# Routed tokens sent to their experts' regions while the gates run, in place of gathers during the routed blocks

## What is computed

```python
t = layernorm(h).reshape(-1, 128)                     # 3136 tokens of 128 numbers
hs = gelu(einsum('td,nfd->ntf', t, sw1) + sb1)        # 2 shared experts, 512 hidden units, every token
shared = einsum('ntf,ndf->td', hs, sw2) + sb2.sum(0)
probs = softmax(t @ gate_w.T + gate_b)                # 8 routed experts
top_v, top_i = top_k(probs, 2)                        # each token goes to 2 of them
hr = gelu(einsum('td,efd->etf', t, rw1) + rb1)
oe = einsum('etf,edf->etd', hr, rw2) + rb2
out = h + shared + einsum('etd,te->td', oe, cw)       # cw: top_v at top_i, else 0
```

## Time and profile before

| | |
|---|---|
| median of the runs | 507.42 us |
| profiled execution | 508.58 us |
| its span (first to last instruction) | 506.8 us |
| PE busy | 386.9 us (76%) |
| DVE busy | 183.7 us (36%) |
| ACT busy | 208.2 us (41%) |
| POOL busy | 193.4 us (38%) |
| mean granted clock of TensorE | 0.891 of full |

### The profile page before, as it was taken

How to read it: one execution, slowest core, us unless ns; L and a number is a source line. 1 busy time by engine, 2 the same in 40 slices (tenths; PEclk the granted TensorE clock), 3 DMA queues, 4 the chain that set the end, 5 groups by cost and what they waited for, 6 DMA issues and landing times.

```text
span 506.8 us, 7360 instructions
## 1 busy us (share of the span) xinstructions
PE 386.9 (76%) x2561; PEld 313.5 (62%) x2561; DVE 183.7 (36%) x564; ACT 208.2 (41%) x423; POOL 193.4 (38%) x254
## 2 busy tenths in 40 slices
PE   0869998999589754999699978888596797696600
PEld 0648666666367643877589677777396496496600
DVE  0661858486930354435861111111021111121146
ACT  2641758463352143766333322424232342342243
POOL 6050262624110025400003466676546666556600
PEclk9995999999779795999988997999798998998955
DMA  9950349300225102110201234344334343444176
GB/s 222 262 160 2 97 120 321 118 1 10 87 77 167 45 1 65 32 34 1 104 38 18 55 130 141 136 141 176 90 119 140 125 147 135 134 130 136 70 210 176
DMA packets 35240, 55.43 MB, mean 109 GB/s; under 512 B 5431, under 2 KB 20397, under 8 KB 35209
## 3 DMA queue, kind: packets, MB, share of 16 engines
q1 hardware_dynamic: 30185, 46.25, 28.7%
q0 software_dynamic: 4480, 8.46, 6.6%
q10 hardware_dynamic: 544, 0.33, 0.3%
HBM read 28.63 MB, written 7.46 MB: 71 GB/s over the span
## 4 chain that ended last, share of the span: by engine, by line
PE 34%; issue 30%; DVE 10%; POOL 6%; POOLq 6%; DMA 5%; another core or an unknown queue 4%; ACT 3%; SPq 1%; DVEq 1%; ACTq 0%
PE bank L1459 12%; PE bank L1481 11%; PE bank L1469 4%; DVE dT L822 3%; DMA out<-osb 2%; DMA gbb<-in_L_ffn_gate_b 2%; ACT gf L765 2%; PE bank L1504 2%; POOLq L598 1%; POOL QT L566 1%; PE bank L1515 1%; POOLq L548 1%; POOL rstd L544 1%; DVE xtok L871 1%
## 5 line engine op out<-in xcount | busy, mean ns | idle before, releaser
L765 ACT ACTIVATE gf<-bank,wba 128x256 f32<-128x256 f32 x128 | 55.2, 474 | 99.0 <-remote 45.5
L610 POOL DMA_INDIRECT xg<-yd,take x64 | 62.5, 977 | 76.9 <-DVE give L1143 57.7
L617 POOL DMA_INDIRECT rd<-og,give x64 | 63.4, 990 | 63.3 <-DVE og L1155 47.1
L1481 PE MATMUL bank<-wbb,gf 128*128 128x128 f32 x512 | 69.1, 293 | 23.2 <-issue 23.1
L1481 PEld LDWEIGHTS bank<-wbb,gf 128*128 128x128 f32 x512 | 65.4, 206 | 25.5 <-issue 25.5
L1459 PE MATMUL bank<-x,wba 128*128 128x256 f32 x256 | 67.5, 406 | 14.0 <-issue 12.5
L1459 PEld LDWEIGHTS bank<-x,wba 128*128 128x128 f32 x256 | 49.4, 205 | 25.2 <-issue 17.0
L765 ACT ACTIVATE gf<-bank,vcol 128x392 f32<-128x392 f32 x64 | 34.7, 589 | 52.2 <-PE bank L1441 33.7
L1155 DVE TENSOR_TENSOR og<-bank,wbb 128x256 f32<-128x256 f32 x32 | 13.6, 424 | 101.8 <-remote 67.1
L1469 PE MATMUL bank<-gf,ws 128*128 128x392 f32 x128 | 45.1, 495 | 0.0
L1254 PE MATMUL bank<-patchT,Wp 128*128 128x392 f32 x96 | 37.4, 515 | 0.0
(11 more groups left out here) (242 smaller groups left out, 617.0 us busy)
## 6 DMA issues: line engine op xcount, KB each, us to landing
wbb<-stb SPq DMA_DIRECT2D x32, 320.0 KB
Xc<-in_x SPq DMA_DIRECT2D x12, 784.0 KB, 6.6
wba<-sta SPq DMA_DIRECT2D x32, 258.0 KB
rk<-rd SPq DMA_DIRECT2D x16, 196.0 KB
Tt<-kpad SPq DMA_DIRECT2D x8, 300.1 KB
raw<-in_L_ffn_rw SPq DMA_DIRECT2D x1, 2048.0 KB, 10.6
yd<-ym SPq DMA_DIRECT2D x8, 196.0 KB
out<-osb SPq DMA_DIRECT2D x8, 196.0 KB
```

Of the source, the lines that this page charges most:

```text
L610: G.indirect_dma_start(out=xg[i % AHEAD][:, t, :], out_offset=None, in_=yd[:, :], in_offset=bass.IndirectOffsetOnAxis(ap=take[:, at:at + 1 ...
L617: G.indirect_dma_start(out=rd[:, :], out_offset=bass.IndirectOffsetOnAxis(ap=give[:, at:at + 1], axis=0), in_=og[i % 2][:, t, :], in_offse ...
L765: nc.scalar.activation(gf[q % 2][:, o, 0:width(q)], bank[o][:, 0:width(q)], ACT.Gelu, bias=bias1(n, o)).then_inc(act_done, 1)
L1481: last = MM(bank[7][:, D * t:D * (t + 1)], gf[q % 2][:, o, 128 * t:128 * (t + 1)], wbb[i % WB][:, o * D:(o + 1) * D], start=o == 0, stop=o ...
```

## The change

The order of units is now all 16 shared units, then the 32 blocks. The sorting is done in four rounds of 8 pairs (`GPP`), in iterations 0 to 3, each as soon as its two groups' gates are through: `choose(g)` finds the two experts of each token from the logits alone, PE's `count(g)` numbers them, and `send(g)`, one iteration later, writes row numbers `xrow`. POOL's `dispatch(g)` then sends the rows of `ym` (now 8 buffers, one per group) to regions of `xd` in DRAM, one region of 3392 rows per expert: 16 indirect DMAs of 98 rows in each round, 64 in all. `number_slots` in iteration 5 finds each block's expert and its first row (`rowint`), and from there on `one_hots`, `invert` and `slot_tokens` work as before for `give` alone, one iteration later than before. SP clears 256 rows behind each region's end (`pad_rows`) and loads each block's 256 consecutive rows with one plain DMA (`load_tokens`). The gathers, the table `take` and the stores to `yd` are gone. The exponential of the gates is moved to iteration 6 and the routed weights to iteration 10 (`shares`).

The diff, cut to its core:

```diff
-LEAD = 12
-EVERY = 6
-ORDER = list(range(LEAD))
-for _i in range(NB):
-    ORDER.append(NSH + _i)
-    if _i % EVERY == EVERY - 1 and LEAD + _i // EVERY < NSH:
-        ORDER.append(LEAD + _i // EVERY)
+ORDER = list(range(NSH + NB))
...
-S_EXP = 4
-S_COUNT = 6
-S_HOT = 5
-S_TURN = 8
+S_NUMBER = 5
+S_HOT = 6
+S_TURN = 9
...
@@ SP
-            for c in range(NG):
-                store_y(c)
+            def load_tokens(i):
+                at = sp_.value_load(rowint[0:1, i:i + 1], min_val=0, max_val=E * TT - BLK)
+                if i == 0:
+                    sp_.wait_ge(st_pad, 16 * E)
+                    for g in range(NGR):
+                        sp_.wait_ge(dispatched[g], 16 * 2 * GPP)
+                if i >= AHEAD:
+                    sp_.wait_ge(tin_done, i - AHEAD + 1)
+                sp_.dma_start(xg[i % AHEAD][:, :, :], xd[bass.ds(at, BLK), :].rearrange("(t p) d -> p t d", t=TILES_OF)).then_inc(ld_xg[i % AHEAD], 16)
...
+            for e in range(E):
+                pad_rows(e)
...
+            for i in range(WB):
+                load_weights(i)
+            for i in range(WB - 1):
+                load_tokens(i)
             for i in range(NB):
-                load_weights(i)
+                if i + WB - 1 < NB:
+                    load_tokens(i + WB - 1)
+                if i + WB < NB:
+                    load_weights(i + WB)
...
@@ POOL, sort_constants
                 G.memset(nothing[:, :], 0.0)
+                G.memset(zrows[:, :, :], 0.0)
+                G.memset(keep[:, :, 1:GPP + 1], 1.0)
+                for i in range(2):
+                    G.memset(run[i][:, :, 0:1], 0.0)
+                for e in range(E):
+                    G.memset(base_of[:, e:e + 1], float(e * TT))
+                G.memset(keep[:, :, 0:1], 0.0)
                 G.memset(allone[:, :], 1.0).then_inc(sort_const, 1)
...
-            def gather(i):
+            def dispatch(g):
+                pool.wait_ge(row_ready, g + 1)
+                for c in range(GC * g, GC * (g + 1)):
+                    for p in range(GP):
+                        for k in range(2):
+                            at = GP * c + p
+                            G.indirect_dma_start(out=xd[:, :], out_offset=bass.IndirectOffsetOnAxis(ap=xrow[:, k, at:at + 1], axis=0),
+                                                 in_=ym[c][:, p, :], in_offset=None).then_inc(dispatched[g], 16)
...
@@ ACT
-                if c >= 4:
-                    act.wait_ge(y_T, c - 3)
-                    act.wait_ge(st_y[c % 4], 16 * (c // 4))
...
-                if q == S_EXP:
+                if q == S_NUMBER + 1:
                     act.wait_ge(lg_ready, 1)
-                    nc.scalar.activation(pr[:, :, :], lg[:, :, :], ACT.Exp).then_inc(exp_ready, 1)
+                    nc.scalar.activation(pr[:, :, :], lg[:, :, :], ACT.Exp)
+                    nc.scalar.activation(cwk[:, :, :], tops[:, :, :], ACT.Exp).then_inc(exp_ready, 1)
...
@@ DVE
-                if q == NG // 2 - 1:
-                    gate_logits()
-                    gate_probs()
-                    gate_second()
-                    sort_places()
+                if 1 <= q <= NGR:
+                    send(q - 1)
+                if q < NGR:
+                    choose(q)
+                if q == S_NUMBER:
+                    number_slots()
...
@@ PE
             def gate(c):
                 pe.wait_ge(yh_ready, c + 1)
+                if c % GC == 0 and c >= GC:
+                    pe.wait_ge(lg_read, c // GC)
+                if c >= 2 * GC and c % GC == 0:
+                    pe.wait_ge(row_ready, c // GC - 1)
...
+                if 1 <= q <= NGR:
+                    count(q - 1)
+                if q == NGR + 1:
+                    count_all()
```

More of the change, by code:

```diff
@@ L169, in tower @@
         rbb = place("rbb", [128, E, D], "w")
+        zrows = place("zrows", [128, TILES_OF, D], "w")
+        ymw = [place(f"ymw{i}", [PAIR, GP, D], "w") for i in range(4)]
         assert end["w"] <= base + SA, (end["w"] - base, SA)
@@ L200, in tower @@
         step256 = place("step256", [PAIR, NCNT], "y")
-        nothing = place("nothing", [PAIR, E * NPAIR], "y")
+        nothing = place("nothing", [PAIR, E], "y")
         idf = place("idf", [PAIR, NPAIR], "y")
@@ L245, in tower @@
         Av = [place(f"Av{i}", [PAIR, NQ, JG], "g", F16) for i in range(2)]
-        ym = [place(f"ym{i}", [PAIR, GP, D], "g") for i in range(4)]
-        first = place("first", [PAIR, E, NPAIR], "g")
+        ym = [place(f"ymg{i}", [PAIR, GP, D], "g") for i in range(4)] + ymw
         more = place("more", [PAIR, E, NCNT], "g")
         owner = place("owner", [1, NB, E], "g")
+        offs = place("offs", [1, NB, E], "g")
+        mine = place("mine", [1, E], "g")
         assert end["g"] <= base_h, (end["g"], base_h)
@@ L302, in tower @@
         ld_wb = [sem(f"ld_wb{i}") for i in range(WB)]
-        gathered = [sem(f"gathered{i}") for i in range(AHEAD)]
+        ld_xg = [sem(f"ld_xg{i}") for i in range(AHEAD)]
         scattered = [sem(f"scattered{i}") for i in range(2)]
@@ L307, in tower @@
         st_zero, st_k, st_out = sem("st_zero"), sem("st_k"), [sem(f"st_out{i}") for i in range(2)]
-        st_y = [sem(f"st_y{i}") for i in range(4)]
+        dispatched = [sem(f"dispatched{i}") for i in range(NGR)]
+        st_pad = sem("st_pad")
         lsrep_ready, par_T, ls_T, vec_T = sem("lsrep_ready"), sem("par_T"), sem("ls_T"), sem("vec_T")
@@ L1094, in sort_places @@
+                V.tensor_tensor(offs[:, :, :], colc[0:1, :].unsqueeze(2).broadcast_to([1, NB, E]),
+                                blocks[0:1, :].unsqueeze(1).broadcast_to([1, NB, E]), ALU.is_ge)
+                dve.drain()
                 V.tensor_reduce(ownsum[:, :], owner[:, :, :], AX.X, ALU.add)
-                V.scalar_tensor_tensor(shiftby[:, :], blocks[:, :], float(BLK), start, ALU.mult, ALU.subtract)
+                V.tensor_tensor(offs[:, :, :], offs[:, :, :], owner[:, :, :], ALU.subtract)
@@ L1106, in sort_places @@
+                dve.drain()
+                for k, of_ in enumerate((eq, tie)):
                     V.tensor_reduce(pos[:, k, :], of_[:, :, :], AX.X, ALU.add)
```

203 lines of the change are left out of this document (118 added, 85 removed).

## The result

The changed kernel takes 619.8 us (median of 4 runs), the kernel before 508.4 (median of 4, taken in turn): a ratio of 1.221, 95% interval 1.210 to 1.231. I had forecast 556 us with a range of 530 to 584. The sign is right, the size is not: 111 us slower instead of 49. The profiled execution took 619.3 us with a span of 617.5.

A forecast was written before the change was run, and what follows sets the result against it. PE bounds the shared stage; the routed stage runs near POOL's rate. First `og` at 293.07 + 20.8 + 12 = 325.9, plus 29 x 6.75 = 195.8, 6.4 and 28.0: span 556.1, predicted 556 us, range 530 to 584.

The forecast's parts named there:

- Part 1: Shared stage: four shared units of 5.2 us moved in front, where PE is the bound, delay everything behind by 20.8 us.
- Part 2: Shared stage: sorting in rounds adds constants, stalls and clock restarts, less the old 3.7 us stall: 12 us in sum.
- Part 3: Shared stage: 64 indirect DMAs on POOL at 1.28 us, 82 us, end near 307, just hidden under the shared units.
- Part 4: Routed stage: SP's queue order allows one block per round trip from `og` to `og`, 6.75 us per lap.
- Every lap throttled: Rival, routed stage: transposes and `down` at the lower clock in each lap, 8.0 us per lap, 593 us; chance 0.08.
- Late dispatch: Rival: slower DVE rounds and 1.5 us per DMA bring block 0 near 326 to 328, 568 to 570 us; chance 0.08.
- the lower bound I had set by rows: Dispatch on POOL: 98 rows cost 98/128 of an indirect DMA's busy part, 67 us for all 64.

The follow-up runs named there:

- e7: The kernel before with all 16 shared units first (LEAD = 16) and nothing else: 526.9 us against 507.8.
- e1: The changed kernel without its dispatch DMAs, blocks' rows read from a small DRAM buffer: 562.4 us (before 474.2).
- e9: The changed kernel without its dispatch DMAs, rows from a small DRAM buffer, on a chip where before takes 509.2 us: 567.1 us.
- e16: The changed kernel with token rows ahead of weights on SP and a one-column memset ahead of every two dispatch DMAs: 470.6 us (before 476.2).
- e8: The changed kernel with each block's token rows loaded ahead of its weights on SP: 534.0 us against 623.7 for the changed kernel.
- e17: The changed kernel, token rows ahead of weights, POOL waiting for PE's up_done ahead of every two dispatch DMAs: 484.4 us (before 509.0).
- e12: The changed kernel, token rows ahead of weights, two 256-column memsets with drains ahead of every two dispatch DMAs: 549.2 us (before 509.2).
- e10: The changed kernel with 64 plain POOL DMAs replacing the indirect dispatch, blocks' rows from a small DRAM buffer: 567.5 us (before 509.2).
- e18: The changed kernel, token rows ahead of weights, one-column memset ahead of every two dispatch DMAs, where before takes 509.0 us: 532.0 us.
- e6: The kernel before as it is, run for its profile: 507.6 us.
- e14: The changed kernel, token rows ahead of weights, one memset with drain ahead of every four dispatch DMAs: 504.1 us (before 476.2).
- e15: The changed kernel, token rows ahead of weights, one memset with drain ahead of every eight dispatch DMAs: 488.3 us (before 476.2).

## Why the prediction was wrong, and what in it held

- **Part 1, four units in front (20.8 us).** Held: 19.1 in e7.
- **Part 2, stalls of the sorting (12 us).** Held. The stall at the gate of group 4 is 6.8 us (I had 5), the one at the count in iteration 4 is 1.8 (2), the one ahead of the `up` of unit 8 is 4.1 (6), all read in e1 and e9, where no dispatch disturbs them, and the 3.73 us of the earlier trace rows are gone. `sort_constants` ends at 197.66 instead of 197.19: 0.5 us, not 1.5. In e9 `og` of block 0 ends at 333.6, and that run reached the gate of group 4 5.7 us later than the profile of the changed kernel did (230.5 against 224.8; in the twenty profiles the first gate starts anywhere from 193.3 to 200.0); that makes 327.9 against my 325.9. Counted from the first gate to the end of that `og`, e9 takes 12.4 us more than e7 (133.5 and 121.1), against my 12.
- **Part 3, the dispatch "hidden under the shared units".** This step failed. Its own arithmetic was right: 1.26 us each, and the last ends at 310 in e16 against 307. What was wrong is that it cost nothing because it was hidden. I priced POOL's time and the wait for its result, and took it without a reason that what POOL does beside PE leaves PE alone. On three of the five chips, and in the first comparison, it doesn't: while POOL issues indirect DMAs without a pause, PE's updates arrive up to 32 us late, and ACT, DVE and then PE stand still. Of the 61.4 us, 2.0 are part 2's. The other 59 came with the two streams: 30.8 and 21.1 us of idle PE, 9.0 us in five smaller waits, and matmuls at half clock (the mean granted clock from 199 to 330 us is 0.69, in e9 0.87). Part 2's two later stalls fall into the same waits, so this isn't a sum to the us.
- **Part 4, the lap (6.75 us).** Held: 6.80. Its parts: 1.23 to the rows' issue (1.19), 2.2 to 2.3 to landing (2.3), `down` at the lower clock in 8 of 29 laps (I had one in four, from a single row, so that this came out is partly luck). e8 removed its cause and it fell to 3.77.
- **The rivals.** Every lap throttled would have been 593 us. The Trainium skill (TensorE: Matmul & The Clock Gate, HAM oscillation — how this bites in real kernels) says that this can happen in such a loop. The rows have `down` at full speed in 21 of 29 laps; PE's wait ahead of the transposes is 2.4 us in the mean and as long in those laps (1.3 to 3.2) as in the 8 slow ones (2.2 to 3.0), so the measurement decides against it here. Late dispatch: not the case; the last DMA starts at 314.08, over 70 us ahead of the first `og`. Nobody among my rivals was the one that came, a stream of transfers off the path that slows the engines on it.

A hint was there. In the trace of before, DVE's `og` and ACT's `gf` had "remote" waits, one of which stands in the earlier trace rows as 5.45 us, and I used that row for its neighbours without asking who on a kernel of one core could be remote. The kernel before was itself about 33 us slower than on the faster chips. A change that gathers so many of POOL's indirect DMAs into two unbroken streams of 40 us had reason to expect the same thing at a larger size.

## What to carry to other kernels

Off the path isn't free: a long run of indirect DMAs on POOL can hold up PE's semaphore updates (on three of five chips here), so pace it by a counter of the engine that must not wait (e17), and read every "remote" in a kernel of one core as such a delay until shown otherwise. In a queue that runs in order, put the transfer whose buffer is free ahead of the one that waits for a result: that alone gave 90 of 624 us (e8). And judge a fix by its stretch in the profile, not by the time alone: e12 was slower than e8 and held the answer.

## What the runs showed of the hardware that I had not expected

- PE's semaphore updates can come 13 to 32 us after the matmul, while POOL issues indirect DMAs back to back for 40 us. They return 4.5 to 5 us after it stops, in the order of the matmuls and 0.05 us apart. Plain DMAs from POOL, 0.56 us each and up to 26.4 us without a pause, don't cause it (e10). The first delay is that of an update 6 us into the stream (231.19, recorded at 234.90), the first long one that of an update 9 us into it (233.90, recorded at 246.94).
- It doesn't occur on every chip: with before at 474 to 476 us, the eight profiles there have not one remote wait, though nearly the same stream runs in e16; that kernel, run on another chip as e18, has waits of up to 38.2 us. The changed kernel itself was never run on a chip of the first kind. The mechanism behind it stays open. So does the least pause that is enough: 2.6 us in each 4.85 (e12) and waits for PE of up to 3.5 us (e17, where late updates were back 1.3 to 2.1 us after POOL's last DMA) are enough, a column's memset in each 2.5 us (e18) is not, and the bursts of 5 and 10 us (e14, e15) ran only where they could tell nothing. The kernel before has bursts of 10 to 12 us, and remote waits of up to 7.7 us (e6).
- Two memsets of 256 columns on POOL with a drain behind each put 2.6 us between two indirect DMAs (e12), three times the 0.9 that I had counted.
- The indirect DMA's busy time is the same for 98 rows and for 128 (0.96 us; 0.98 to 0.99 in the kernel before), so the lower bound I had set by rows was too low.
